# Products with v in four runs of two sets of heads a batch instead of eight runs of one

## The chip, the cores and the metric

The kernel runs on one core of one Trainium2 chip. The metric is device time of one execution in microseconds (us). The engines of the core are named as in the profile: PE is TensorE (PEld its loading of weights), DVE is VectorE, ACT is ScalarE, POOL is GpSimd, SP is the engine that issues the DMAs.

## The reference

Sixteen independent graphs ("batches") of 512 nodes with 128 features go through two layers, all in float32:

```python
h = relu(layernorm(x))                                 # per node
q, k, v = split(h @ W_qkv + b_qkv)                     # 8 heads of 16
scores = where(adj, q @ k.T / 4, -inf)                 # 512 x 512 a head
x = x + (softmax(scores) @ v) @ W_out + b_out          # layer 0
h = relu(layernorm(x))
z_l, z_g, v = h @ Wl, h @ Wg, h @ Wv
A_l = relu(cosine(z_l)); A_g = exp(-|z_g - z_g'|^2/2)  # zero diagonal
K = 0.9 * rownorm(A_l * adj) + 0.1 * rownorm(A_g * adj)
out = x + (K @ v) @ Wo                                 # layer 1
```

The change concerns `softmax(scores) @ v` of layer 0.

## The kernel before

**One time axis of slots.** The program of every engine is written out by one loop `for s in slots`. A batch takes 32 slots for its attention tiles (8 heads times 4 blocks of 128 nodes), and the other stages stand in a table `AT` by name, as slot numbers counted from the batch's own slot 0; batch b's are 32 b later. The table runs from slot -37 to slot 100, so in the steady state three or four batches are in work at a time. This text counts slots modulo 32, "slot 0" to "slot 31", and calls 32 slots a round. Within a slot the order of the stages on an engine is that of the code. Each engine is a queue in program order; the semaphores (`reached(...)`) say what it waits for. [...]

**A tile of attention.** In each slot PE makes one tile of scores (L725, read by DVE at L1021 for the maxima of the rows) and one tile of the same scores turned, 128 keys by 512 queries, of 21 slots ago (L733; in every slot divisible by 4 the mask is first put into that bank by L721). ACT takes the exponential of the turned tile into `probs_t` (L1186), and POOL multiplies three of four such tiles by the mask (L587). There are two banks for the scores and two for the turned tiles, so both matmuls of a slot wait until DVE and ACT have read those of two slots before.

**Sets and products with v.** Four turned tiles, of the four heads of a group and one block of keys, make a set. There are eight sets a batch: four blocks of keys for each of the two groups of heads. `attend` multiplies a set by v: four matmuls, one for each head, which write 32 of the 128 partitions each of the bank `pv_bank` and add up over the four sets of a group. In float32 each is two matmul instructions in the trace, so a set is 8 rows of L747. `probs_t` keeps six sets (`KEPT`). After the fourth set of a group ACT copies the bank (`pv_copy`, L1229). In the table, "pv" stands at eight slots of a batch, four apart: modulo 32 these are slots 28, 0, 4, 8 for the first group and 12, 16, 20, 24 for the second.

**Other work in these slots on PE.** Slot 28: `mix_cos` of the second layer (L761) and `yT` (L779), which turns the scaled y after DVE's `y_scale` (L1118). Slot 30: `mix_rbf` (L761), after DVE's `adj_rbf` (L1053), and `attn` (L895). Slot 0: `max_turn` (L854). Slot 4: nothing else. Slots 5, 6, 8, 10: `z` (L756), whose banks are those that DVE's `out` (L1062 to L1076) reads. Slots 8 and 10: q and k (L756), which ACT and DVE split into two parts (L1248, L1095). Slot 12: `zgT` (L779). Slot 13: nothing else. Slots 14 to 17: `col`, `zlT`, `rbf`, `cos`, from where DVE's masks of layer 1 start (`cos_read`, L1039). Slot 20: nothing else. Slot 27: `y` (L779), after DVE's first `y_scale`.

**The last batch** has its own slots for the second layer (`AT_LAST`); "pv" is not among them.

Of the kernel before, what the change touches and what calls it, by code (L numbers as in the profile page):

```python
# [53 lines left out]
AT = {  # L54

    "hT": (-26,), "q": (-24,), "k": (-22,), "v": (-13,), "max_turn": (17, 32),
    "pv": (28, 32, 36, 40, 44, 48, 52, 56), "y": (54, 59), "yT": (60,), "attn": (62,), "h2T": (66,),
    "z": (69, 70, 72, 74), "zgT": (76,), "col": (78,), "zlT": (79,), "rbf": (79, 83, 85, 87),
    "cos": (81, 83, 86, 90), "mix_cos": (92, 95, 97, 98), "mix_rbf": (94, 95, 97, 98),

# [37 lines left out]
def reached(engine, signal, batch, nth=None):  # L98
    count = (batch * signal.per + (signal.per if nth is None else nth)) * signal.step
    if count > 0:  # L100
        engine.wait_ge(signal.sem, count)


def graph_blocks(nc, x, adj, w_qkv, b_qkv, w_out, b_out, w_l, w_g, w_v, w_o, out):
# [3 lines left out]
    T = N // P  # L108
    GROUPS = 2
    HG = H // GROUPS  # L110
# [38 lines left out]
    def kept(batch, k):  # L149

        return (SETS * batch + k) % KEPT
# [8 lines left out]
    with ExitStack() as ctx:  # L160
        def sb(name, shape, dt=F32):
            return ctx.enter_context(nc.sbuf_tensor(name, shape, dt))

        def bank(name):
            return ctx.enter_context(nc.psum_tensor(name, [P, 512], F32))

        def signal(name, per=1, step=1):
            return Signal(ctx.enter_context(nc.semaphore(name)), per, step)
# [52 lines left out]
        v_cols = sb("v_cols", [P, 3, T, H, 32])  # L221
# [4 lines left out]
        probs_t = sb("probs_t", [P, KEPT, HG, N])  # L226
# [3 lines left out]
        yT = sb("yT", [P, N])  # L230
# [40 lines left out]
        pv_bank = bank("pv")  # L271
# [71 lines left out]
        pv_filled = signal("pv_filled", SETS)  # L343
# [322 lines left out]
        def _(pe):  # L666
# [67 lines left out]
                              qk_rows[row:row + ROWS + 2, b % 2, 0, h // 2, :], start=w not in by_pe, stop=True,  # L734
                              tile_position=(row, 0)).then_inc(turned_filled.sem, 1)

            def attend(b, k):
                g, j = divmod(k, T)
                ends = (k + 1) * HG
                reached(pe, probs_masked, b, sum(w < ends for w in by_pool))  # L740
                if by_pe:
                    reached(pe, probs_ready, b, 1 + max(w for w in by_pe if w < ends))
                if j == 0:
                    reached(pe, v_ready, b)
                    reached(pe, pv_copied, b, g)
                for hl in range(HG):
                    last = pe.matmul(pv_bank[32 * hl:32 * (hl + 1), :], v_cols[:, b % 3, j, g * HG + hl, :],  # L747
                                     probs_t[:, kept(b, k), hl, :], start=(j == 0), stop=(j == T - 1),
                                     tile_position=(0, 32 * hl))
                last.then_inc(pv_filled.sem, 1)  # L750

            def split_product(dst, left, right, before_rest=None):
                for part, (a, c) in enumerate(((0, 0), (0, 1), (1, 0))):
# [5 lines left out]
            def mix(bank_, adjacency, n, right, rows):  # L759
                for m in rows:  # L760
                    last = pe.matmul(bank_, adjacency[:, m, n * P:(n + 1) * P], right(m), start=(m == 0),  # L761
                                     stop=(m == T - 1))
                return last
# [10 lines left out]
            def rbf_half(batch, n):  # L774
                return mix_bank(batch, n)[:, 256:256 + D + 1]
# [6 lines left out]
            for s in slots:  # L782
# [11 lines left out]
                if hit := due(s, "pv"):  # L794
                    attend(*hit)

                if hit := due(s, "cos"):
                    b, m = hit
# [8 lines left out]
                if hit := due(s, "rbf"):  # L807
                    b, m = hit
# [10 lines left out]
                if hit := due(s, "mix_cos"):  # L819
                    b, n = hit  # L820
# [13 lines left out]
                if hit := due(s, "mix_rbf"):  # L834
                    b, n = hit
# [4 lines left out]
                    else:  # L840
                        m = n
                        reached(pe, rbf_ready, b, m + 1)
                        for n in range(T):
                            last = mix(rbf_half(b, n), adj_rbf, n, v_of_rbf, [m])
# [3 lines left out]
                if hit := due(s, "max_turn"):  # L848
                    b, g = hit
# [7 lines left out]
                if hit := due(s, "hT"):  # L857
                    b, _ = hit
# [3 lines left out]
                for which, name in enumerate(("q", "k")):  # L862
                    if hit := due(s, name):
                        b, _ = hit
# [7 lines left out]
                if hit := due(s, "v"):  # L872
                    b, _ = hit
                    reached(pe, hT_ready, b)
                    bank_free(pe, work_turns, b, "v")
                    for t in range(T):
                        last = pe.matmul(work_bank[:, t * P:(t + 1) * P], hT[:, t * P:(t + 1) * P],
                                         wqkv_sb[:, 2 * D:3 * D], start=True, stop=True)
                    last.then_inc(v_filled.sem, 1)
                if hit := due(s, "y"):  # L880
                    b, g = hit
# [3 lines left out]
                if hit := due(s, "yT"):  # L885
                    b, _ = hit
# [3 lines left out]
                if hit := due(s, "attn"):  # L890
                    b, _ = hit
                    reached(pe, yT_ready, b)
                    bank_free(pe, work_turns, b, "attn")
                    for t in range(T):
                        last = pe.matmul(work_bank[:, t * P:(t + 1) * P], yT[:, t * P:(t + 1) * P],  # L895
                                         wout_sb[:, :], start=True, stop=True)
                    last.then_inc(attn_filled.sem, 1)
                if hit := due(s, "h2T"):
                    b, _ = hit
# [3 lines left out]
                if hit := due(s, "z"):  # L903
                    b, t = hit
# [13 lines left out]
                if hit := due(s, "zgT"):  # L918
                    b, _ = hit
# [3 lines left out]
                if hit := due(s, "col"):  # L923
                    b, _ = hit
# [3 lines left out]
                if hit := due(s, "zlT"):  # L928
                    b, _ = hit
# [377 lines left out]
```

## Time and profile before

| | |
|---|---|
| three runs | 848.60, 844.22, 848.76 us (median 848.6) |
| profiled execution | 850.23 us, its span 848.5 us, 1.7 us around it |
| busy share of the span | PE 91%, DVE 79%, POOL 74%, ACT 69% |
| mean granted clock of TensorE | 0.971 of full speed |

All engines work side by side, and none is busy all the time. A busy PE in the profile counts matmuls whose ends are modelled, so the share alone does not tell what ends the time; the chain of waits does, and it goes through several engines in turn. The rounds of the steady state are alike: from about 140 us on, a round takes 48.25 us (from the matmul L725 of slot 28 at 385.28 us to that at 433.52 us), and the same waits come back in each.

### The profile page before, as it was taken

How to read it: one execution, taken by the hardware profiler on the slowest of the kernel's cores; microseconds unless marked ns; L12 is line 12 of the kernel's file. 1: busy time of each engine (PE TensorE's matmuls, PEld its weight loads, DVE VectorE, ACT ScalarE, POOL GpSimd, SP SyncE). 2: the span in 40 equal slices, each digit the busy share in tenths (PEclk: the TensorE clock that was granted, in tenths of full speed). 3: DMA queues.
4: the chain of work that ended last, by engine and by line, in shares of the span. 5: the costliest groups of instructions: out<-in, count | busy, mean ns of one | idle time of the engine just before them, and what ended most of it. 6: DMA issues, size and time to landing. Idle time of an engine off the chain costs nothing.

```text
span 848.5 us, 15592 instructions
## 1 busy us (share of the span) xinstructions
PE 774.0 (91%) x4736; PEld 410.8 (48%) x4736; DVE 672.5 (79%) x1957; ACT 589.5 (69%) x1230; POOL 624.4 (74%) x707
## 2 busy tenths in 40 slices
PE   4888799999999999999999999999999999989886
PEld 3322235546454554646454554645455454536366
DVE  6677659788887979788797979888796978877266
ACT  4337676876868686776868687776868677575832
POOL 3249786887869697886969788786969788685911
PEclk9859889999999999999999999999999999999999
DMA  2211111120201121020112112020112111100000
GB/s 87 69 56 58 33 57 33 32 70 20 82 16 55 33 65 38 29 73 20 53 30 69 33 37 65 20 82 20 51 32 70 32 34 57 32 2 2 13 1 26
DMA packets 43059, 35.76 MB, mean 42 GB/s; under 512 B 6625, under 2 KB 36834, under 8 KB 42978
## 3 DMA queue, kind: packets, MB, share of 16 engines
q1 hardware_dynamic: 42978, 34.76, 13.5%
q8 instruction: 41, 0.67, 0.3%
q14 instruction: 40, 0.33, 0.1%
HBM read 17.70 MB, written 16.78 MB: 41 GB/s over the span
## 4 chain that ended last, share of the span: by engine, by line
PE 59%; DVE 19%; ACT 12%; issue 7%; POOL 1%; DVEq 0%; POOLq 0%; ACTq 0%
PE adj L761 14%; PE score L725 11%; PE pv L747 10%; PE adj L756 7%; DVE scrap L1021 7%; PE work L779 6%; ACT probs_t L1186 4%; DVE adj_cos L1039 3%; PE turned L721 3%; DVE rbf_arg L1048 3%; DVE adj_rbf L1053 2%; PE work L756 2%; ACT zl_square L1264 2%; PE work L895 2%; ACT z L1257 2%
## 5 line engine op out<-in xcount | busy, mean ns | idle before, releaser
L587 POOL TENSOR_TENSOR probs_t<-probs_t,keep_t 128x512 int32<-128x512 int32 x384 | 488.7, 1300 | 70.8 <-ACT probs_t L1186 70.6
L1186 ACT ACTIVATE probs_t<-turned,exp_scale 128x512 f32<-128x512 f32 x512 | 345.1, 695 | 94.0 <-PE turned L733 91.2
L1021 DVE CUSTOM_DVE_ANT_0 scrap<-score,mask_add 128x512 f32<-128x512 f32 x512 | 340.3, 682 | 56.9 <-PE score L725 56.6
L725 PE MATMUL score<-qk_rows 48*128 48x512 f16 x512 | 193.4, 395 | 26.9 <-ACT probs_t L1186 20.3
L733 PE MATMUL turned<-qk_rows 50*128 50x512 f16 x512 | 192.6, 395 | 1.1 <-ACT probs_t L1186 1.1
L747 PE MATMUL pv<-probs_t,v_cols 128*32 128x512 f32 x1024 | 140.3, 621 | 1.3 <-POOL probs_t L587 1.3
L725 PEld LDWEIGHTS score<-qk_rows 48*128 48x128 f16 x512 | 44.1, 93 | 184.0 <-issue 114.9
L761 PE MATMUL adj<-v_cos,adj_cos 128*128 128x129 f32 x480 | 69.3, 286 | 0.4 <-DVE out_sb L1076 0.4
L761 PEld LDWEIGHTS adj<-v_cos,adj_cos 128*128 128x128 f32 x480 | 58.1, 190 | 21.9 <-issue 21.2
L761 PE MATMUL adj<-z,adj_rbf 128*128 128x129 f32 x480 | 64.7, 278 | 0.0
L1053 DVE SCALAR_TENSOR_TENSOR adj_rbf<-rbf_exp,mask_t 128x512 f32<-128x512 f32 x64 | 62.7, 982 | 1.0 <-ACT rbf_exp L1220 1.0
L756 PE MATMUL adj<-zgT_parts 128*128 128x512 f32 x186 | 59.2, 427 | 2.8 <-DVE zgT_parts L1139 1.0
L756 PE MATMUL adj<-zlT_parts 128*128 128x512 f32 x186 | 60.0, 431 | 1.7 <-DVE adj_cos L1039 0.6
L761 PEld LDWEIGHTS adj<-z,adj_rbf 128*128 128x128 f32 x480 | 58.1, 191 | 6.0 <-issue 6.0
L1220 ACT ACTIVATE rbf_exp<-rbf_arg,rbf_bias 128x512 f32<-128x512 f32 x64 | 45.9, 718 | 18.8 <-DVE rbf_arg L1048 16.9
L1048 DVE TENSOR_TENSOR rbf_arg<-adj,col_term 128x512 f32<-128x512 f32 x62 | 42.5, 685 | 18.2 <-PE adj L756 17.7
L721 PE MATMUL turned<-bar_t,ident_b 128*128 128x512 bf16 x128 | 50.7, 396 | 2.3 <-ACT probs_t L1186 1.4
L598 POOL TENSOR_SCALAR var_eps<-moments 128x4 f32<-128x4 f32 x16 | 3.6, 228 | 60.7 <-DVE moments L996 60.7
L733 PEld LDWEIGHTS turned<-qk_rows 50*128 50x128 f16 x512 | 43.7, 93 | 7.2 <-ACT probs_t L1186 3.6
L1039 DVE SCALAR_TENSOR_TENSOR adj_cos<-adj,mask_t 128x512 f32<-128x512 f32 x62 | 42.5, 686 | 4.5 <-PE adj L756 3.7
L756 PE MATMUL adj<-wz_parts,h2T_parts 128*128 128x384 f32 x180 | 44.6, 356 | 0.1
L1195 ACT ACTIVATE x_norm<-x_sb,ln_shift,rstd 128x128 f32<-128x128 f32 x64 | 26.4, 483 | 23.7 <-issue 18.6
(170 smaller groups left out, 1123.0 us busy)
## 6 DMA issues: line engine op xcount, KB each, us to landing
q_dram<-split SPq DMA_DIRECT2D x48, 128.0 KB, 2.1
k_dram<-split SPq DMA_DIRECT2D x48, 128.0 KB, 2.2
qk_rows<-q_dram SPq DMA_DIRECT2D x64, 96.0 KB, 2.7
qk_rows<-k_dram SPq DMA_DIRECT2D x64, 96.0 KB, 2.7
x_sb<-in_x_dram SPq DMA_DIRECT2D x16, 256.0 KB, 3.1
out_dram<-out_sb SPq DMA_DIRECT2D x15, 256.0 KB, 2.5
qk_rows<-max_rows SPq DMA_DIRECT2D x128, 2.0 KB
adj_sb<-in_adj_dram SPq DMA_DIRECT2D x1, 256.0 KB, 3.0
```

What stands on the lines that cost most here:

```text
L587: pool.tensor_tensor(tile, tile, keep_t[:, w // HG % T, :], ALU.mult).then_inc(probs_masked.sem, 1)
L721: pe.matmul(turned_bank[w % 2][:, :], ident_b[:, :], bar_t[:, w // HG % T, :], start=True, stop=False)
L725: pe.matmul(score_bank[u % 2][:, :], qk_rows[row:row + ROWS, b % 2, 0, h // 2, t * P:(t + 1) * P], qk_rows[row:row + ROWS, b % 2, 1, h // ...
L733: pe.matmul(turned_bank[w % 2][:, :], qk_rows[row:row + ROWS + 2, b % 2, 1, h // 2, j * P:(j + 1) * P], qk_rows[row:row + ROWS + 2, b % 2, ...
L747: last = pe.matmul(pv_bank[32 * hl:32 * (hl + 1), :], v_cols[:, b % 3, j, g * HG + hl, :], probs_t[:, kept(b, k), hl, :], start=(j == 0), ...
L756: last = pe.matmul(dst, left(a), right(c), start=(part == 0), stop=(part == 2))
L761: last = pe.matmul(bank_, adjacency[:, m, n * P:(n + 1) * P], right(m), start=(m == 0), stop=(m == T - 1))
L1021: dve.tensor_tensor_reduce(scrap[:, u % 2, :], score_bank[u % 2][:, :], mask_add[:, t, :], -1.0 / MAX_UNIT, 3.0e38, ALU.add, ALU.min, neg_ ...
L1039: dve.scalar_tensor_tensor(adj_cos[:, m, :], cos_bank(b, m)[:, :], 0.0, mask_t[:, m, :], ALU.max, ALU.mult).then_inc(cos_ready.sem, 1)
L1048: dve.tensor_tensor(rbf_arg[:, m % 2, :], rbf_bank(b, m)[:, :], col_term[:, :], ALU.add).then_inc(rbf_arg_ready.sem, 1)
L1053: dve.scalar_tensor_tensor(adj_rbf[:, m, :], rbf_exp[:, m % 2, :], 1.0, mask_t[:, m, :], ALU.min, ALU.mult).then_inc(rbf_ready.sem, 1)
L1186: act.activation(probs_t[:, kept(b, k), w % HG, :], turned_bank[w % 2][:, :], ACT.Exp, scale=exp_scale[:, 0:1]).then_inc(probs_ready.sem, 1)
```

## The change

"pv" stands at four slots of a batch instead of eight, and each call of `attend` multiplies two sets. The slots that stay are those of the second set of each pair, 0, 8, 16 and 24 modulo 32; slots 28, 4, 12 and 20 lose their set. The waits are those of the second set, and are made ahead of the first. The signal `pv_filled` still goes up once a set. Lines of the changed kernel below this place stand three lines further down (L747 becomes L750).

```diff
-    "pv": (28, 32, 36, 40, 44, 48, 52, 56), "y": (54, 59), "yT": (60,), ...
+    "pv": (32, 40, 48, 56), "y": (54, 59), "yT": (60,), ...
...
-            def attend(b, k):
-                g, j = divmod(k, T)
-                ends = (k + 1) * HG
+            def attend(b, pair):
+                g = 2 * pair // T
+                ends = 2 * (pair + 1) * HG
                 reached(pe, probs_masked, b, sum(w < ends for w in by_pool))
                 if by_pe:
                     reached(pe, probs_ready, b, 1 + max(w for w in by_pe if w < ends))
-                if j == 0:
+                if 2 * pair % T == 0:
                     reached(pe, v_ready, b)
                     reached(pe, pv_copied, b, g)
-                for hl in range(HG):
-                    last = pe.matmul(pv_bank[32 * hl:32 * (hl + 1), :], v_cols[:, b % 3, j, g * HG + hl, :],
-                                     probs_t[:, kept(b, k), hl, :], start=(j == 0), stop=(j == T - 1),
-                                     tile_position=(0, 32 * hl))
-                last.then_inc(pv_filled.sem, 1)
+                for k in (2 * pair, 2 * pair + 1):
+                    j = k % T
+                    for hl in range(HG):
+                        last = pe.matmul(pv_bank[32 * hl:32 * (hl + 1), :], v_cols[:, b % 3, j, g * HG + hl, :],
+                                         probs_t[:, kept(b, k), hl, :], start=(j == 0), stop=(j == T - 1),
+                                         tile_position=(0, 32 * hl))
+                    last.then_inc(pv_filled.sem, 1)
```

PE before, slots 4 to 8 of a round: `score` and `turned` are the two tiles of a slot, `turned<-bar_t` opens slots 4 and 8, `wz_parts` is `z`, `x_norm` is `hT`, and `wqk_parts` in slot 8 is q.

```order
L721 MATMUL turned<-bar_t,ident_b 128x512
L725 MATMUL score<-qk_rows 128x512
L733 MATMUL turned<-qk_rows 128x512
L747 MATMUL pv<-probs_t,v_cols 32x512 x4
L725 MATMUL score<-qk_rows 128x512
L733 MATMUL turned<-qk_rows 128x512
L756 MATMUL adj<-wz_parts,h2T_parts 128x384 x3
```

PE now at the same place, from slot 4 to the start of `z` in slot 5:

```order
L721 MATMUL turned<-bar_t,ident_b 128x512
L725 MATMUL score<-qk_rows 128x512
L733 MATMUL turned<-qk_rows 128x512
L725 MATMUL score<-qk_rows 128x512
L733 MATMUL turned<-qk_rows 128x512
L759 MATMUL adj<-wz_parts,h2T_parts 128x384 x3
```

The tiles of slots 4 and 5 now follow each other with nothing between them; the set that stood there is in slot 8, ahead of q.

PE now in slot 8 and after it: the run of two sets, q, `z`, and the tiles of slot 9.

```order
L721 MATMUL turned<-bar_t,ident_b 128x512
L725 MATMUL score<-qk_rows 128x512
L733 MATMUL turned<-qk_rows 128x512
L750 MATMUL pv<-probs_t,v_cols 32x512 x8
L759 MATMUL work<-hT_parts,wqk_parts 128x512 x3
L759 MATMUL adj<-wz_parts,h2T_parts 128x384 x3
```

Where `x8` stands there was `x4`; all else in the slot has kept its order, and stands behind four matmuls more.

PE before, slots 12 to 14: `work<-ident,z` is `zgT`, `work<-ident,rbf_bias` is `col` of slot 14.

```order
L733 MATMUL turned<-qk_rows 128x512
L747 MATMUL pv<-probs_t,v_cols 32x512 x4
L779 MATMUL work<-ident,z 128x128 x4
L725 MATMUL score<-qk_rows 128x512
L733 MATMUL turned<-qk_rows 128x512
L725 MATMUL score<-qk_rows 128x512
L733 MATMUL turned<-qk_rows 128x512
L779 MATMUL work<-ident,rbf_bias 128x128 x4
```

PE now at the same place:

```order
L733 MATMUL turned<-qk_rows 128x512
L782 MATMUL work<-ident,z 128x128 x4
L725 MATMUL score<-qk_rows 128x512
L733 MATMUL turned<-qk_rows 128x512
L725 MATMUL score<-qk_rows 128x512
L733 MATMUL turned<-qk_rows 128x512
L782 MATMUL work<-ident,rbf_bias 128x128 x4
```

Four matmuls are gone from slot 12; they are in slot 16, behind that slot's tiles and ahead of the `cos` of slot 17.

## Rows read from the trace of the kernel before

**Rows 1.** The page, parts 4 and 5: the chain by line; L747's group.

```profile
PE adj L761 14%; PE score L725 11%; PE pv L747 10%; PE adj L756 7%; DVE scrap L1021 7%; PE work L779 6%; ACT probs_t L1186 4%; DVE adj_cos L1039 3%; PE turned L721 3%; DVE rbf_arg L1048 3%; DVE adj_rbf L1053 2%; PE work L756 2%; ACT zl_square L1264 2%; PE work L895 2%; ACT z L1257 2%
...
L747 PE MATMUL pv<-probs_t,v_cols 128*32 128x512 f32 x1024 | 140.3, 621 | 1.3 <-POOL probs_t L587 1.3
```

**Rows 2.** Chain of waits, 384 to 436 us: start, length (us), what.

```profile
384.30 0.14 issue
...
385.67 0.99 PE pv L747 x8
...
393.55 1.00 PE pv L747 x8
...
400.60 0.99 PE pv L747 x8
...
405.04 0.99 PE pv L747 x8
...
406.96 0.03 ACT split L1248
...
417.32 0.99 PE pv L747 x8
...
419.57 0.69 DVE adj_cos L1039
...
432.11 0.44 DVE y_sb L1118
```

**Rows 3.** PE in order of time: start, length (us), what, [idle before <-releaser].

```profile
387.59 0.60 PE L779 MATMUL work<-ident,y_sb 128*128 128x128 f32 x4
...
388.66 1.16 PE L761 MATMUL adj<-z,adj_rbf 128*128 128x129 f32 x8
...
393.48 1.07 PE L747 MATMUL pv<-probs_t,v_cols 128*32 128x512 f32 x8
394.36 0.22 PE L854 MATMUL work<-ident_h,max_parts 128*32 128x128 f16 x1
...
403.30 0.77 PE L756 MATMUL adj<-wz_parts,h2T_parts 128*128 128x384 f32 x3
...
405.96 0.96 PE L756 MATMUL work<-hT_parts,wqk_parts 128*128 128x512 f32 x3
...
414.16 0.37 PE L725 MATMUL score<-qk_rows 48*128 48x512 f16 x1 [1.24 <-ACT probs_t L1186]
...
418.25 0.39 PE L725 MATMUL score<-qk_rows 48*128 48x512 f16 x1
...
430.17 0.39 PE L725 MATMUL score<-qk_rows 48*128 48x512 f16 x1
```

**Rows 4.** DVE in order of time, the same round.

```profile
386.31 0.42 DVE L1118 TENSOR_TENSOR y_sb<-work,inv_den 128x256 f32<-128x256 f32 x1
...
387.26 0.68 DVE L1053 SCALAR_TENSOR_TENSOR adj_rbf<-rbf_exp,mask_t 128x512 f32<-128x512 f32 x1
...
402.59 0.35 DVE L1076 SCALAR_TENSOR_TENSOR out_sb<-adj,inv_degree,half_sum 128x128 f32<-128x128 f32 x1
...
431.22 0.68 DVE L1021 CUSTOM_DVE_ANT_0 scrap<-score,mask_add 128x512 f32<-128x512 f32 x1
```

**Rows 5.** POOL in order of time, the same round.

```profile
391.05 1.28 POOL L587 TENSOR_TENSOR probs_t<-probs_t,keep_t 128x512 int32<-128x512 int32 x1
```

**Rows 6.** Windows of the round before: length, busy time (count) by engine, PEclk, DMA.

```profile
363.40:366.60 3.20, 1.96 (x12) 1.02 (x12) 1.91 (x5) 2.63 (x8) 2.96 (x5) 0.99 0.63 205
366.60:370.00 3.40, 3.40 (x14) 1.50 (x16) 2.29 (x5) 2.31 (x4) 3.23 (x7) 0.50 0.00 0
```

**Rows 7.** PE in order of time, the same stretch of that round.

```profile
364.94 0.37 PE L725 MATMUL score<-qk_rows 48*128 48x512 f16 x1 [1.24 <-ACT probs_t L1186]
...
370.58 0.39 PE L725 MATMUL score<-qk_rows 48*128 48x512 f16 x1
```

More of the change, by code:

```diff
@@ L56 @@
     "hT": (-26,), "q": (-24,), "k": (-22,), "v": (-13,), "max_turn": (17, 32),
-    "pv": (28, 32, 36, 40, 44, 48, 52, 56), "y": (54, 59), "yT": (60,), "attn": (62,), "h2T": (66,),
+    "pv": (32, 40, 48, 56), "y": (54, 59), "yT": (60,), "attn": (62,), "h2T": (66,),
     "z": (69, 70, 72, 74), "zgT": (76,), "col": (78,), "zlT": (79,), "rbf": (79, 83, 85, 87),
```

## The prediction

> **What bounds the kernel now.** I read the chain of waits first, then each engine in order of time over one round (slot 28 at 385.28 us to the next slot 28 at 433.52 us, 48.25 us), then the windows.
>
> The chain by line gives the products with v 10% of the span, 85 us [rows 1]. A set stands on the chain with 0.99 us [rows 2], and there are 1024 / 8 = 128 sets [rows 1], so 127 us if all stood there. About 86 of 128 do, some five in eight, and the chain of the round shows which: those at 385.67, 393.55, 400.60, 405.04 and 417.32 us, that is of slots 28, 0, 4, 8 and 16 [rows 2]. The sets of slots 12, 20 and 24 stand beside the chain. What takes their place is to be seen in the same view: from 406.96 us the chain is ACT (the split of q, then z, exponentials and squares one after the other) until PE's tile of slot 14 at 414.16 us, for which PE had stood idle 1.24 us [rows 2, 3]; from 419.57 us it is DVE, from the first `cos_read` to `y_scale` at 432.11 us [rows 2]; then PE again, from slot 27 to q of slot 8. So the round is a relay: PE in slots 27 to 8, ACT in 8 to 13, PE in 14 to 17, DVE in 17 to 27.
>
> **The change part by part.** I follow one round and keep an account of how much later (+) or earlier (-) the chain is than before.
>
> *A run of two sets.* No run of two is in the trace. A set that is followed by a matmul of its own tile shape (`max_turn`, 128*32) gives way after 394.36 - 393.48 = 0.88 us; the other sets, followed by another shape, after 0.99 us [rows 2, 3]. The second set could cost nothing if it lay wholly beside the first, and 0.99 us if it gained nothing; I take 0.88, the nearest row. A doubled slot is then 0.88 us longer, and a slot that loses its set 0.99 us shorter, if PE has something to do.
>
> *Pair of slots 28 and 0.* Without its set, PE reaches `yT` 0.99 us earlier, at 386.60. But y comes from DVE, at 386.31 + 0.42 = 386.73 [rows 4], and from an engine's end to PE's start the chain has 0.14 us [rows 2]: 386.87 instead of 387.59, -0.72. `mix_rbf` of slot 30 would then start at 387.94, but `adj_rbf` ends at 387.26 + 0.68 = 387.94 and lets it go at 388.08 instead of 388.66 [rows 3, 4]: -0.58. DVE runs on from slot 25 without a gap there, so it does not come earlier. In slot 0 POOL's last mask ends at 391.05 + 1.28 = 392.33 [rows 5]; PE is there at 393.48 - 0.58 = 392.90, no wait. Then the second set: -0.58 + 0.88 = **+0.30**.
>
> *Pair of slots 4 and 8.* Slot 4 is left with its tiles. PE would now reach the second `z` (slot 6) 0.7 us earlier, but its bank is read by `out`, which ends at 402.59 + 0.35 = 402.94 [rows 4] and is itself 0.30 later, since DVE had waited for the score of slot 3. `z` starts at 402.94 + 0.30 + 0.14 = 403.38 instead of 403.30 [rows 3]: +0.08. Of 0.99 us taken away, PE gets 0.22. In slot 8 q then starts at +0.08 + 0.88 = **+0.96**, 406.92 instead of 405.96 [rows 3]. The split of q on ACT and all that follows it in ACT's queue, up to the exponential that frees the tile of slot 14, comes 0.96 later.
>
> *Pair of slots 12 and 16.* The set of slot 12 lay in time in which PE then waits for ACT anyway. Taking it out makes the wait of 1.24 us [rows 3] about 2.2 us, and the tile of slot 14 comes no earlier. The second set in slot 16 stands ahead of `cos`, on the chain: +0.88, together **+1.84**.
>
> *Pair of slots 20 and 24.* From `cos_read` to `y_scale` DVE is the chain, so taking the set of slot 20 out gives nothing. The second set in slot 24 lets the score of slot 25 start at 430.17 + 0.88 = 431.05 [rows 3] instead; it takes 0.39, so DVE can't start on it before 431.44, where it started at 431.22 [rows 4]: +0.22, and `y_scale`, behind it in DVE's queue, as much. Together **+2.06 us a round**. ACT's copy of the bank comes 0.88 later and pushes the exponentials of slots 25 and 26; that falls behind the wait for `y_scale` in slot 28, where PE waits anyway.
>
> *Waits that the change adds or moves.* The wait for masks is that of the second set, which was met at the same slot before; sets waited 1.3 us for POOL in all [rows 1]. The first set's tiles are held four slots longer, and ACT wants their place of six back thirteen slots or more after the new run: no wait. No DMA is moved; those of the maxima follow `max_turn`, later by as much as the chain.
>
> Fifteen rounds at 2.06 us are 30.9 us. The sixteenth is split between start and end, where fewer batches overlap; its four pairs lie between -0.11 and +0.88 each, -0.4 to +3.5 us, and I count nothing.
>
> *The clock.* In the round before, PE stood idle 1.24 us ahead of slot 14 [rows 7], was busy 1.96 of 3.20 us around it, and the granted clock then was 0.50, 1.2 instead of 2.4 GHz, for the next 3.40 us [rows 6]. From the tile of slot 14 to that of slot 17 that round took 370.58 - 364.94 = 5.64 us, the round at full clock 418.25 - 414.16 = 4.09 [rows 3, 7]: a fall costs 1.55 us, and this stretch is PE's part of the chain. The round of rows 3 had the same idle time and no fall, so before it stands at the edge. With about 2.2 us of idle time at this place I expect it in most rounds, and count ten more: 15.5 us (none to fifteen more: 0 to 23 us). The Trainium skill ("TensorE: Matmul & The Clock Gate", Part 1) says that the clock is granted by how busy PE has lately been, and these rows agree; by that rule the idle time that a longer wait adds is paid twice.
>
> Sum: 850.2 us of the profiled execution (848.5 of span and 1.7 around it) + 30.9 + 15.5 = 896.6. That execution lies 1.6 us above the median of the runs, so in their terms 848.6 + 46.4 = **895 us**.
>
> **The rivals.**
>
> *Only the waits, no more falls of the clock:* 848.6 + 30.9 = 880. For it: in the round of the other rows the same wait of 1.24 us passed at full clock [rows 3]. Against: the wait grows by three quarters.
>
> *The waits are smaller than I think:* sets taken from slots 28 and 4, which are on the chain, pay in full (0.99 against 0.88, -0.11 each), and only the sets that move from beside the chain onto it cost: 0.88 + 0.22 - 0.22 = 0.88 a round, 13 us, 862. For it: a DVE that is not held up may run ahead. Against: `y_scale` and `out` end when they end, in queues without gaps.
>
> *Every moved set costs its full price:* 4 x 0.88 x 15 = 53, with 23 of clock 925. For it: each doubled slot is followed by work that others wait for. Against: the slack computed in slots 28, 4 and 25.
>
> *Faster:* one place and price, the exit from a run of sets into another shape of tile. Four exits fewer a batch, 64 in all, at 0.99 - 0.88 = 0.11 us [rows 2, 3] are 7 us: 842. It decides if PE has its next operands ready wherever a set is taken away, so in slots 28, 4, 12 and 20 alike. The Trainium skill ("TensorEngine Tiling (Array Packing)", Key Properties) says that a change of tiling mode drains the engine; the 0.11 us agrees, and by this rule alone the time would be 842. Against it: three of eight sets, with two of those taken away, lie where PE waits for ACT or DVE, and a drain saved there is waited away.
>
> **How the numbers follow.** Forecast 0.55 (895, own range 884 to 912), waits alone 0.20 (880, 872 to 888), smaller waits 0.10 (862), full price 0.07 (925), faster 0.05 (842), about no change 0.03. A measurement of this kernel tells half a per cent, 4 us, from no change. The range 863 to 914 leaves out the two ends, half of the smaller waits and the edges: under 0.2. Faster 0.05, within half a per cent 0.02, slower 0.93.
>
> **What would show it.** In the profile of the changed kernel: a set's rows in pairs, some 1.87 us from a run's start to the next shape; PE's idle time ahead of the tile of slot 14 near 2.2 us and again due to ACT's exponential; a wait for `y_sb` at `yT` and for `out_sb` ahead of the second `z`; the chain still through DVE from `cos_read` to `y_scale`; a round of about 50.3 us, 51.9 with a fall of the clock, and a mean clock near 0.94. It would be wrong if the round came out under 49 us, if the sets of slots 0 or 8 came off the chain, or if PE's idle time in slot 13 stayed at 1.2 us.

## The result, and the profile after

The changed kernel takes 896.0 us (median of four runs, 893.98 to 897.98) where the kernel before, run beside it, takes 847.7 (844.22 to 848.76): a ratio of 1.060, 95% interval 1.056 to 1.063, 48.3 us slower. Forecast were 895 us. The sum was near, in part by luck: the waits of a round were taken 0.6 us too high, and the start and end of the execution, which hold more waits than were counted for them, made it good, as the traces and runs below show. The profiled execution took 894.96 us, its span 893.2, 44.7 us more than that of before, at a mean clock of 0.951 (0.971 before).

First the page of the changed kernel: the clock in 40 slices, the chain by engine and by line, and the group of the products with v.

```profile
PEclk9968999999999999999999999999999999989899
...
PE 72%; ACT 12%; issue 6%; DVE 5%; POOL 1%; SPq 0%; DMA 0%; DVEq 0%; POOLq 0%; ACTq 0%
...
L750 PE MATMUL pv<-probs_t,v_cols 128*32 128x512 f32 x1024 | 127.1, 616 | 2.1 <-POOL probs_t L587 2.1
```

The same two lines of the page of the kernel before, which do not stand above:

```profile
PEclk9859889999999999999999999999999999999999
...
PE 59%; DVE 19%; ACT 12%; issue 7%; POOL 1%; DVEq 0%; POOLq 0%; ACTq 0%
```

DVE has left the chain (19% to 5%), and PE has taken its place. The products with v hardly wait for POOL (2.1 us in all, 1.3 in [rows 1]). The slices of the clock hide what the windows below show: most read 9, though the clock falls in every steady round.

The chain of waits of the changed kernel, one round: start, length (us), what.

```profile
410.04 1.85 PE pv L750 x16
...
422.28 1.85 PE pv L750 x16
...
425.06 0.03 ACT split L1251
...
436.95 1.85 PE pv L750 x16
...
440.05 0.70 DVE adj_cos L1042
...
449.10 1.85 PE pv L750 x16
```

All four runs of two sets stand on the chain whole, 7.4 us a round, where five sets with 0.99 us stood there before [rows 2]. The `adj_cos` at 440.05 is the only work of DVE left on the chain of the round; before, DVE was the chain from there to `y_scale`. ACT's stretch from the split of q to the tile of slot 14 is still there.

PE of the changed kernel in order of time, from one slot 28 to the next: start, length (us), what, [idle before <-releaser].

```profile
402.64 0.39 PE L725 MATMUL score<-qk_rows 48*128 48x512 f16 x1 [0.42 <-ACT probs_t L1189]
...
402.96 1.16 PE L764 MATMUL adj<-v_cos,adj_cos 128*128 128x129 f32 x8
404.03 0.63 PE L782 MATMUL work<-ident,y_sb 128*128 128x128 f32 x4
...
409.97 1.92 PE L750 MATMUL pv<-probs_t,v_cols 128*32 128x512 f32 x16
411.71 0.22 PE L857 MATMUL work<-ident_h,max_parts 128*32 128x128 f16 x1
...
418.33 0.37 PE L725 MATMUL score<-qk_rows 48*128 48x512 f16 x1 [0.39 <-ACT probs_t L1189]
...
420.44 0.77 PE L759 MATMUL adj<-wz_parts,h2T_parts 128*128 128x384 f32 x3
...
422.21 1.92 PE L750 MATMUL pv<-probs_t,v_cols 128*32 128x512 f32 x16
424.06 0.96 PE L759 MATMUL work<-hT_parts,wqk_parts 128*128 128x512 f32 x3
...
430.00 0.63 PE L782 MATMUL work<-ident,z 128*128 128x128 f32 x4 [0.90 <-DVE split L1098]
...
432.25 0.37 PE L725 MATMUL score<-qk_rows 48*128 48x512 f16 x1 [1.25 <-ACT probs_t L1189]
...
438.74 0.39 PE L725 MATMUL score<-qk_rows 48*128 48x512 f16 x1
...
453.84 0.39 PE L725 MATMUL score<-qk_rows 48*128 48x512 f16 x1 [0.42 <-ACT probs_t L1189]
```

The round is 453.84 - 402.64 = 51.20 us, 2.95 more than the 48.25 before. Twelve rounds of the trace are alike in this; together they take 614.4 us, the same twelve of the kernel before 579.7. That is 34.7 of the 44.7 us by which the span grew; the other 10.0 lie in the start and the end. A run of two is left after 424.06 - 422.21 = 1.85 us, and after 1.74 when `max_turn` follows: the second set costs 0.86. Idle time that was not there before stands ahead of the tile of slot 5 (0.39, at 418.33), which waits for an exponential of ACT, and ahead of `zgT` in slot 12 (0.90), which waits until DVE's split of k has read the bank that `zgT` writes. The 1.25 ahead of slot 14 are what they were [rows 3].

The 0.42 ahead of the tile of slot 28 are for the most part no wait. The mask matmul L721 of that slot stands in them; its own row is missing, as are 74 of 128 in this trace, while its weight load is there:

```profile
L721 PEld LDWEIGHTS turned<-bar_t,ident_b x128: 95/96/151, 51.9 to 850.7; 128*128 128x128 bf16 x128
L721 PE MATMUL turned<-bar_t,ident_b x54: 376/390/634, 52.0 to 850.7; 128*128 128x512 bf16 x54
...
402.30 0.10 PEld L721 LDWEIGHTS turned<-bar_t,ident_b 128*128 128x128 bf16 x1 [0.33 <-DVE neg_max L1024]
```

The work before it ends at 402.22, so what PE waits there is about 0.1 us.

From the tile of slot 14 to that of slot 17 it is 438.74 - 432.25 = 6.49 us against 4.09 [rows 3], and the windows of the changed kernel tell why: length, busy time (count) of PE, PEld, DVE, ACT, POOL, then the clock, DMA share and GB/s.

```profile
429.00:433.20 4.20, 2.05 (x16) 1.13 (x14) 3.11 (x9) 3.68 (x13) 3.00 (x5) 1.00 0.50 164
433.20:436.60 3.40, 3.40 (x13) 1.96 (x12) 1.50 (x5) 2.15 (x4) 2.90 (x5) 0.50 0.12 33
436.60:440.00 3.40, 3.40 (x24) 1.08 (x24) 2.05 (x7) 1.57 (x3) 2.94 (x5) 1.00 0.01 2
```

PE is busy 2.05 of 4.20 us, and then has half its clock for 3.40 us, in the stretch in which it is the chain. This comes in each of the twelve rounds, 51.2 us apart; in the profile of the kernel before it comes in one of the twelve. Of the 2.40 us, 0.88 are the added set and 1.52 the clock.

By slot, a round of the changed kernel against one before, median of the steady rounds (us; a slot's time runs from its turned tile on PE to that of the next slot, and slots that are not named differ by less than 0.05): 28: -0.89, 0: +0.86; 4: -0.54, 6: +0.32, 7: +0.11, 8: +0.85; 12 to 14: 0; 15: +1.51, 16: +0.89; 20: -0.41, 23: -0.21, 24: +0.86, 25: -0.34, 27: -0.06. These numbers are called the account below.

### The profile page after: what moved, and what is told of

It is laid out like the page before. It is cut to its first block, busy times and chain, and to the rows that moved or that the text cites. A ratio compares the mean times of both kernels' runs of the same rounds, so it can differ in the third digit from the quotient of the medians.

```text
span 893.2 us, 15452 instructions
## 1 busy us (share of the span) xinstructions
PE 772.3 (86%) x4660; PEld 428.9 (48%) x4736; DVE 664.5 (74%) x1957; ACT 591.2 (66%) x1230; POOL 618.4 (69%) x707
## 4 chain that ended last, share of the span: by engine, by line
PE 72%; ACT 12%; issue 6%; DVE 5%; POOL 1%; SPq 0%; DMA 0%; DVEq 0%; POOLq 0%; ACTq 0%
PE adj L759 15%; PE pv L750 14%; PE adj L764 13%; PE score L725 12%; PE work L782 7%; ACT probs_t L1189 4%; PE work L759 2%; PE turned L721 2%; DVE scrap L1024 2%; PE work L898 2%; ACT zl_square L1267 2%; ACT z L1260 1%; PE work L880 1%; PE turned L733 1%; DVE adj_cos L1042 1%
## 5 line engine op out<-in xcount | busy, mean ns | idle before, releaser
L587 POOL TENSOR_TENSOR probs_t<-probs_t,keep_t 128x512 int32<-128x512 int32 x384 | 481.9, 1278 | 125.1 <-ACT probs_t L1189 123.5
L750 PE MATMUL pv<-probs_t,v_cols 128*32 128x512 f32 x1024 | 127.1, 616 | 2.1 <-POOL probs_t L587 2.1
L759 PE MATMUL adj<-zgT_parts 128*128 128x512 f32 x186 | 68.2, 481 | 1.3 <-DVE zgT_parts L1142 1.0
L750 PEld LDWEIGHTS pv<-probs_t,v_cols 128*32 128x32 f32 x1024 | 27.4, 112 | 59.4 <-issue 55.4
L1056 DVE SCALAR_TENSOR_TENSOR adj_rbf<-rbf_exp,mask_t 128x512 f32<-128x512 f32 x64 | 53.1, 832 | 1.0 <-ACT rbf_exp L1223 1.0
L759 PEld LDWEIGHTS adj<-zgT_parts 128*128 128x128 f32 x186 | 36.5, 219 | 19.7 <-issue 9.7
```

What stands on the lines that cost most here:

```text
L587: pool.tensor_tensor(tile, tile, keep_t[:, w // HG % T, :], ALU.mult).then_inc(probs_masked.sem, 1)
L759: last = pe.matmul(dst, left(a), right(c), start=(part == 0), stop=(part == 2))
L1056: dve.scalar_tensor_tensor(adj_rbf[:, m, :], rbf_exp[:, m % 2, :], 1.0, mask_t[:, m, :], ALU.min, ALU.mult).then_inc(rbf_ready.sem, 1)
```

## The experiments

All experiments have a table `PV_RUNS`, which says what sets each call of `attend` multiplies, and `attend` loops over that run as the changed kernel loops over its pair. Ratios are against the kernel before on the same chip, which took 845.7 to 846.3 us there.

### The four pairs, each alone

```diff
-    "pv": (28, 32, 36, 40, 44, 48, 52, 56),
...
+    "pv": (32, 36, 40, 44, 48, 52, 56),    # p1_pair_28_0:   runs (0, 1) (2,) (3,) (4,) (5,) (6,) (7,)
+    "pv": (28, 32, 40, 44, 48, 52, 56),    # p2_pair_4_8:    runs (0,) (1,) (2, 3) (4,) (5,) (6,) (7,)
+    "pv": (28, 32, 36, 40, 48, 52, 56),    # p3_pair_12_16:  runs (0,) (1,) (2,) (3,) (4, 5) (6,) (7,)
+    "pv": (28, 32, 36, 40, 44, 48, 56),    # p4_pair_20_24:  runs (0,) (1,) (2,) (3,) (4,) (5,) (6, 7)
```

Slots 28 and 0:

> Only the sets of slots 28 and 0 become one run in slot 0; the other six sets stay single. By the account of the prediction (y_scale and adj_rbf hold PE in slots 28 and 30) the round grows by 0.30 us, 15 rounds, so 852 us against 847.7. By the round measured with all four pairs (slots 28 to 1 took 9.23 us before and after) it costs nothing: 848. If the four pairs share the loss of 48 us evenly: 860. The clock should fall no more often than before.

848.56 us, ratio 1.002 (0.9999 to 1.005); the round 48.42, that is +0.20: slot 28 -0.68, slot 0 +0.86. The added set costs its 0.86, the one taken away pays 0.68.

Slots 4 and 8:

> Only the sets of slots 4 and 8 become one run in slot 8. By the account of the prediction +0.66 us a round: 858 us. By the round measured with all four pairs (slot 1 to q of slot 8 took 0.74 us longer) 859. If the loss is shared evenly: 860. If the drain saved is what counts: 846. PE's idle time ahead of slot 14 stays 1.24 us, so the clock falls in few rounds.

861.5 us, ratio 1.017 (1.012 to 1.021); the round 48.97, +0.75: slot 4 -0.54, 6 +0.31, 7 +0.11, 8 +0.85. Of the set taken away 0.12 us is left by slot 8. The account of the changed kernel has the same four numbers.

Slots 12 and 16:

> Only the sets of slots 12 and 16 become one run in slot 16. The set of slot 12 lies where PE waits for ACT. By the account of the prediction +0.88 us a round, and PE's idle time ahead of slot 14 grows to some 2.2 us, so the clock falls in nearly every round at 1.5 us each: 847.7 + 13 + 22 = 883 us. Without falls of the clock 861. If the loss is shared evenly: 860.

883.34 us, ratio 1.043 (1.037 to 1.049); the round 51.22, +3.0. It alone makes the clock fall in eleven of the twelve rounds, and longer than in the changed kernel. Windows of this experiment, the same columns:

```profile
423.20:426.60 3.40, 1.72 (x11) 0.74 (x9) 2.20 (x6) 3.40 (x13) 2.36 (x3) 0.97 0.32 111
426.60:430.00 3.40, 2.93 (x10) 1.66 (x11) 1.77 (x5) 2.14 (x5) 3.07 (x8) 0.50 0.42 125
430.00:433.40 3.40, 3.40 (x17) 1.51 (x20) 2.35 (x5) 1.78 (x3) 2.19 (x4) 0.53 0.00 0
```

By slot: 14 +0.68, 15 +1.53, 16 +1.32, 23 -0.21, 25 -0.34. Take away the set (0.88), and 2.65 us of clock are left, one time and three quarters the 1.52 of the changed kernel. That the time is the 883 of the expectation is luck: the clock costs more than the 1.5 us that it had, and slots 23 and 25 give 0.55 back, which it had not. The first two `adj_rbf` after `cos_read` take 1.31 and 0.68 us here; why that matters is shown below.

Slots 20 and 24:

> Only the sets of slots 20 and 24 become one run in slot 24. By the account of the prediction (DVE is the chain there, the score of slot 25 comes too late for it) +0.22 us a round: 851 us. By the round measured with all four pairs (slots 17 to 28 took 0.17 us less) 845. If the loss is shared evenly: 860. The clock should fall no more often than before.

855.7 us, ratio 1.010 (1.006 to 1.014); the round 48.71, +0.49: 20 -0.40, 22 +0.38, 24 +0.86, 25 -0.34, 27 -0.06. No account had this: that of the prediction had too little, and 860 was too much. In the changed kernel the same slots make -0.17. The set taken out of slot 20 gives nothing here, as the prediction had it, for nearly all of its 0.40 goes into slot 22 again; the second set in slot 24 costs 0.46 where 0.22 were foreseen. PE and DVE of this experiment show a wait for DVE in slot 22:

```profile
425.20 0.63 PE L783 MATMUL work<-ident,pv_sb 128*128 128x128 f32 x4 [0.19 <-DVE v_cols L1109]
```

```profile
421.20 1.56 DVE L1057 SCALAR_TENSOR_TENSOR adj_rbf<-rbf_exp,mask_t 128x512 f32<-128x512 f32 x1
...
423.29 1.16 DVE L1057 SCALAR_TENSOR_TENSOR adj_rbf<-rbf_exp,mask_t 128x512 f32<-128x512 f32 x1
```

The four alone add up to 4.44 us a round, together they cost 2.95. Two causes for the difference stood to be tried, the clock and these long `adj_rbf`.

### The clock held up

Five matmuls on constants fill PE's idle time ahead of the tile of slot 14, once in the changed kernel, once in the kernel before. They write a bank that is free there, and nothing reads what they write.

```diff
+    "warm": (77,),
...
+                if (hit := due(s, "warm")) and hit[0] < B - 1:
+                    for _ in range(5):
+                        pe.matmul(adj_bank[0][:, :], ident_b[:, :], mask_add[:, 0, :], start=True, stop=True)
```

> The changed kernel with five extra matmuls a batch in slot 13, of constants into a bank that nobody reads before it is written anew; they lie in PE's wait for ACT ahead of the tile of slot 14 (about 1.1 of 1.25 us) and change no result. If the falls of the clock cost 1.5 us in each round, as the stretch from slot 14 to 17 has it, the clock stays up, the round takes 49.7 us instead of 51.2 and the kernel about 896 - 22 = 874 us. If the falls only fill time in which PE would wait anyway, 896.

874.23 us, ratio 1.034 (1.031 to 1.037). The page's clock, and PE at the place:

```profile
PEclk9968999999999999999999999999999999999999
```

```profile
420.89 0.63 PE L783 MATMUL work<-ident,z 128*128 128x128 f32 x4 [0.90 <-DVE split L1102]
421.50 0.37 PE L726 MATMUL score<-qk_rows 48*128 48x512 f16 x1
421.51 0.39 PE L734 MATMUL turned<-qk_rows 50*128 50x512 f16 x1
421.83 1.25 PE L803 MATMUL adj<-mask_add,ident_b 128*128 128x512 bf16 x5
423.14 0.37 PE L726 MATMUL score<-qk_rows 48*128 48x512 f16 x1
```

With the 1.25 us filled, and the 0.90 still there, the clock falls in no steady round, and the round is 49.67 us; the rest of the account is unchanged. The falls of the changed kernel so cost 896.0 - 874.2 = 21.8 us.

> The kernel before with the same five matmuls in slot 13. Its clock falls there in one or two rounds of an execution, at 1.5 us each: 1 to 3 us less than before, 843 to 845 against 845.9, which may be no difference that can be measured. If the extra matmuls delay the tile of slot 14, slower by up to 15 x 0.5 us.

842.64 us, ratio 0.996 (0.994 to 0.998), 3.7 us less: the falls of the kernel before were worth so little, since few of its rounds had one.

The four times together part the loss. With the clock held in both kernels the change costs 874.2 - 842.6 = 31.6 us, which are waits; the falls that it adds cost 21.8 - 3.7 = 18.1 us. By the spans of the four profiled executions (893.2, 869.3, 848.5, 841.4) it is 27.9 and 16.8; the runs of the changed kernel with the clock held spread from 871.0 to 877.7 us, and its profile is of the shortest. Of the 27.9 us of waits the twelve alike rounds hold 17.2 (596.1 against 578.9 us, 1.44 a round). The other 10.7 lie in the start and the end; what makes them was not taken apart, and as the two kernels differ there by 6.7 us at half clock, a part of them can be clock.

### Who makes DVE late

Taking two of POOL's multiplications by the mask out, those beside the first two `adj_rbf` after `cos_read`, from the kernel before, and from that with the pair 20 and 24 alone (these two kernels leave out a part of the computation):

```diff
-    by_pool = [w for w in range(SLOTS) if w % HG not in MASK_BY_PE]
+    by_pool = [w for w in range(SLOTS) if w % HG not in MASK_BY_PE and w not in (29, 30)]
```

DVE and POOL of the kernel before, the stretch that the experiment is about:

```profile
422.62 1.56 DVE L1053 SCALAR_TENSOR_TENSOR adj_rbf<-rbf_exp,mask_t 128x512 f32<-128x512 f32 x1
...
424.71 1.15 DVE L1053 SCALAR_TENSOR_TENSOR adj_rbf<-rbf_exp,mask_t 128x512 f32<-128x512 f32 x1
```

```profile
422.34 1.29 POOL L587 TENSOR_TENSOR probs_t<-probs_t,keep_t 128x512 int32<-128x512 int32 x1
423.57 1.74 POOL L587 TENSOR_TENSOR probs_t<-probs_t,keep_t 128x512 int32<-128x512 int32 x1
425.55 1.46 POOL L587 TENSOR_TENSOR probs_t<-probs_t,keep_t 128x512 int32<-128x512 int32 x1 [0.24 <-ACT probs_t L1186]
```

> The kernel before, with two of POOL's multiplications by the mask left out in each batch (the tiles of slots 18 and 19, so one block of keys of two heads stays unmasked): those that run beside DVE's first two adj_rbf, which take 1.56 and 1.15 us there instead of 0.69. If POOL's work stretches them, they fall to 0.7 us; DVE's stretch is 1.3 us shorter, and PE, whose own waits in slots 22 to 27 come to some 0.6 us, gains about 0.6 us a round: 837 us. If DVE's stretch doesn't bound the round: 846, with the short adj_rbf.

837.45 us, ratio 0.991 (0.988 to 0.994); the round 47.66: slot 23 -0.21, slot 25 -0.34. DVE of this experiment:

```profile
413.60 0.68 DVE L1057 SCALAR_TENSOR_TENSOR adj_rbf<-rbf_exp,mask_t 128x512 f32<-128x512 f32 x1
...
415.03 0.69 DVE L1057 SCALAR_TENSOR_TENSOR adj_rbf<-rbf_exp,mask_t 128x512 f32<-128x512 f32 x1
```

> The run of two in slot 24 alone (855.7 us), with the same two multiplications left out. In the kernel with all four pairs this pair cost nothing, alone it costs 0.49 us a round, by a wait of 0.38 us in slot 22. If the difference is the stretched adj_rbf, this wait goes and slot 23 gets shorter too: some 0.6 us a round less, 846 us. If not, 856.

847.65 us, ratio 1.003 (0.9997 to 1.005); the round 48.08. The +0.38 of slot 22 is gone and the -0.21 of slot 23 is there, as in the changed kernel. There DVE reads:

```profile
443.10 1.30 DVE L1056 SCALAR_TENSOR_TENSOR adj_rbf<-rbf_exp,mask_t 128x512 f32<-128x512 f32 x1
...
444.94 0.68 DVE L1056 SCALAR_TENSOR_TENSOR adj_rbf<-rbf_exp,mask_t 128x512 f32<-128x512 f32 x1
```

The rounds of the kernel before, of p4, x1 and x2 are 48.23, 48.72, 47.67 and 48.08 us. So the two masks cost 0.56 us a round without the pair and 0.64 with it, and the pair 20 and 24 costs 0.49 with the masks and 0.41 without them: it has a price of its own, which the masks do not explain. What the changed kernel has beside it is the gain of x1: its slots 23 and 25 read -0.21 and -0.34 as there, and its `adj_rbf` take 1.30 and 0.68 us. The pair 12 and 16, which alone has the same two steps and 1.31 and 0.68, brings that gain. With the two steps counted there, the pair 20 and 24 costs -0.41 + 0.86 - 0.06 = +0.39 in the changed kernel, as it does in x2.

A fall of the clock brings the same gain to the kernel before. In its one steady round with a fall [rows 6, 7] slots 15 and 16 take 1.55 us longer, slots 23 and 25 take 0.54 less, and `adj_rbf` 1.32 and 0.68 us. The tile of slot 28 ahead of that round stands here:

```profile
336.06 0.39 PE L725 MATMUL score<-qk_rows 48*128 48x512 f16 x1
```

The round is 385.28 - 336.06 = 49.22 us, 0.99 more than those beside it and not 1.55. In x1, where there is nothing left to give back, the one steady round with a fall takes 49.20 instead of 47.67 us, 1.53 more.

### Is there a better place for a set?

If sets only have to stand where PE waits anyway, moving one from the chain into such a place should pay. Set 3 from slot 8 to slot 9, where PE waits for ACT's split; set 5 from slot 16 to slot 20, where DVE seemed to be the chain:

```diff
-    "pv": (28, 32, 36, 40, 44, 48, 52, 56),
...
+    "pv": (28, 32, 36, 41, 44, 48, 52, 56),    # f1_set3_slot9
+    "pv": (28, 32, 36, 40, 44, 52, 56),        # f2_set5_slot20: runs (0,) (1,) (2,) (3,) (4,) (5, 6) (7,)
```

> The kernel before with the set of slot 8 one slot later, in slot 9, so behind q instead of ahead of it; all runs single. If ACT's stretch from q to the tile of slot 14 is the chain, as read from the chain of waits, it starts 0.99 us earlier, PE has room for the set ahead of k, and the round shrinks by up to 0.99 us: 833 us. If PE's own work is what bounds the round, moving a set by one slot changes nothing: 846.

841.49 us, ratio 0.995 (0.992 to 0.997); the round 47.97, 0.26 less, a quarter of the full gain. By slot: 8 -0.35, 9 +1.10, 10 -0.63, 13 -0.21, 23 -0.18. The chain of this experiment names what is late next:

```profile
403.75 0.49 ACT hT L1240
...
404.33 0.70 DVE hT_parts L1092
405.04 0.14 issue
405.17 0.94 PE work L760 x3
```

q now waits for its own operand. The set of slot 8 had covered that.

> The kernel before with the set of slot 16 moved to slot 20, where it makes a run of two with the set that stands there. So a run of two sets in a slot beside the chain, and a set less on PE's stretch ahead of the cos of slot 17, from where DVE is the chain. If that reading holds, up to 0.9 us a round less: 833 us. If runs of two cost by themselves, or DVE's stretch isn't the chain: 846 or more.

846.1 us, ratio 1.001 (0.999 to 1.004); the round 48.37, +0.14. The gain did not come: slot 16 -0.51, 17 +0.28, 19 +0.08, 20 +0.86, 23 -0.21, 25 -0.34. PE of this experiment at slot 17:

```profile
414.58 0.39 PE L726 MATMUL score<-qk_rows 48*128 48x512 f16 x1 [0.42 <-DVE neg_max L1025]
...
415.17 0.96 PE L760 MATMUL adj<-zlT_parts 128*128 128x512 f32 x3 [0.21 <-DVE zlT_parts L1148]
```

PE got half of the set back in slot 16, having to wait for DVE, and lost more of it in slot 17. In slot 20, where I had taken it to be free, the set cost 0.86, of which slots 23 and 25 gave 0.55 back: PE, being later, waited less for DVE there.

Last, two changes on top of set 3 in slot 9: three constant matmuls in slot 13, and with them one of the masks beside `adj_rbf` given from POOL to PE.

```diff
-    by_pe = [w for w in range(SLOTS) if w % HG in MASK_BY_PE]
-    by_pool = [w for w in range(SLOTS) if w % HG not in MASK_BY_PE]
+    by_pe = [w for w in range(SLOTS) if w % HG in MASK_BY_PE or w in (30,)]
+    by_pool = [w for w in range(SLOTS) if w not in by_pe]
```

> The set of slot 8 in slot 9 and three extra matmuls in slot 13, masks as before: what the candidate has without the mask by PE. The round of the set alone was 47.97 us against 48.22, without a fall of the clock in the steady part; so 841, or 0.5 us a round more if the extra matmuls delay the tile of slot 14: 848.

841.19 us, ratio 0.994 (0.992 to 0.997): the filler alone adds nothing measurable to f1.

> Candidate for a faster kernel: the set of slot 8 in slot 9, three extra matmuls in slot 13 to hold the clock, and the mask of the tile of slot 19 put in by PE (0.32 us more there) instead of POOL, so that POOL is done 1.3 us earlier beside adj_rbf. The set alone gave 841.5. DVE's stretch gets about 0.5 us shorter, PE's work 0.3 us longer: 838 us. If PE's work is what counts there: 845.

838.76 us, ratio 0.990 (0.988 to 0.994): 1% faster than the kernel before, and the fastest of those that leave nothing of the computation out. Against the kernel without the mask by PE, that mask costs 0.42 us in slot 18 and gives 0.15 and 0.34 back in slots 19 and 25; the round is 47.87 instead of 47.97 us.

## Why the prediction came out, step by step

The prediction had four pairs and a clock. A round (us), after less before; the steps of slots 23 and 25 have a row of their own:

| | predicted | alone | in the changed kernel |
|---|---|---|---|
| 28 and 0 | +0.30 | +0.20 | -0.03 |
| 4 and 8 | +0.66 | +0.75 | +0.74 |
| 12 and 16, the second set | +0.88 | +0.88 (taken) | +0.89 |
| slots 23 and 25 | nothing | -0.55 (with 12 and 16) | -0.55 |
| 20 and 24 | +0.22 | +0.49 | +0.39 |
| sum of the waits | 2.06 | 1.77 | 1.44 |
| clock, of a round with a fall | 1.55 | 2.65 | 1.51 |

**Right: the cost of a second set.** 0.88 was taken, and 0.85 to 0.89 was measured in slots 0, 8, 16 and 24, alone and together.

**Right: slots 4 and 8.** DVE of the changed kernel has the `out` that the second `z` waits for:

```profile
419.94 0.35 DVE L1079 SCALAR_TENSOR_TENSOR out_sb<-adj,inv_degree,half_sum 128x128 f32<-128x128 f32 x1
```

It ends at 420.29, and `z` starts 0.15 us later, at 420.44, as foreseen; before, `z` started 0.36 us after it [rows 3, 4]. The wait of 0.39 for ACT's exponential in slot 5 stands ahead of it and was not foreseen. Of 0.99 us PE kept 0.12 instead of 0.22.

**Right in the sum, wrong in the place: slots 12 and 16.** The prediction let the idle time ahead of slot 14 grow to 2.2 us, and named an idle time that stays at 1.2 as a sign of being wrong. It stayed at 1.25. What grew is the wait ahead of `zgT`, 0.90 us, in slot 12; the sum of the two, 2.15, is what was foreseen. The set of slot 12 had stood where DVE's split of k was awaited. Since ACT sets when slot 14 starts, the time is the same by both.

**Missing: DVE's `adj_rbf` beside POOL's masks.** The prediction took DVE's stretch from `cos_read` to `y_scale` to be as long as before, whatever PE does. It is not: two `adj_rbf` there took 1.56 and 1.15 us beside POOL's masks, and where the stretch starts at another time against the masks they take 1.30 and 0.68. This is worth 0.55 us a round, nearly all of the 0.62 by which the sum was too high. It is also a good part of why DVE left the chain, which the prediction had it keep: DVE has 19% of the chain before, 10% in x1 without the two masks, 13% in p4 with the pair 20 and 24, 5% in x2 with both, and 5% in the changed kernel.

**Wrong in size: slots 28 and 0.** "DVE runs on from slot 25 without a gap there, so it does not come earlier" holds for the pair alone, where +0.20 was measured, and fails in the changed kernel, where DVE comes 0.2 us earlier against PE for its shorter `adj_rbf`. The foreseen wait for `y_sb` at `yT` is there, but small: `yT` stands 1.07 us behind `mix_cos`, which took 1.00 before. ACT's copy of the bank pushes the exponential of slot 28, which costs about 0.1 us; the prediction laid that beside a larger wait for `y_scale`.

**Wrong in size: slots 20 and 24.** "From `cos_read` to `y_scale` DVE is the chain, so taking the set of slot 20 out gives nothing" holds for the pair alone. There the second set cost 0.46 instead of 0.22. With the shorter `adj_rbf` the first half fails too: taking the set out gives 0.41, and the second set costs its full 0.86. Why the 0.22 was too small by half when the pair stands alone was not taken apart.

**The clock: price right, count near.** A fall cost 1.52 us in the changed kernel where 1.55 was taken from one row [rows 3, 7]. That row's round lost 0.99 only, as the gain in `adj_rbf` came with the fall; in the changed kernel that gain is there with or without it, so the falls cost their full price. Ten more were counted. Between 120 us and the last 10 us of the execution the clock falls 15 times in the profile of the changed kernel and 3 times in that of before, 12 more. The runs have 18.1 us for it against 15.5.

**The whole sum.** The waits were put at 30.9 us, and the runs have 31.6 (27.9 by the spans). That they agree is luck: over the twelve alike rounds the prediction has 24.7 us and the traces 17.2. The start and the end, for which it has the other three rounds, 6.2 us, hold 10.7 by the spans. "I count nothing" for what lies outside fifteen rounds failed by 4 us by the spans and 8 by the medians; the rounds were overrated by 7.5.

Of the rivals, waits alone is what c1 brings about: 874, against 842.6 + 30.9 = 873.5 over a kernel before with its clock held too. Smaller waits (862) was right that DVE may run ahead, and wrong that slot 4 pays in full. Full price (925) fell, as only the pair 12 and 16 cost it in full. The faster one, four exits saved, fell: the exits are saved (1.85 us for two sets instead of 2 x 0.99), but slots 4, 12 and 20 pay back 0.12, nothing and 0.41 of the set that they lose.

## What to carry to other kernels

A short matmul group that depends on nothing recent can hide a wait where it stands. In this kernel, bunched sets cost their full time in the new place (0.85 to 0.89 us each time), and the place that they left paid back between nothing and 0.89, depending on what was late next. Before moving one, look in the order of time for that second wait, on each engine, and for the idle time that is left to PE: two waits of about one us a round were enough to pay for them again with half the clock. Where a sum comes near the result, check its terms by slot before trusting them; here the waits of the alike rounds were 7 us too high, and the start and the end made it good. And count how many rounds are alike before multiplying: there were twelve, not fifteen.

## What the runs showed of the hardware that was not expected

- DVE's `adj_rbf`, which reads two operands from SBUF, takes 0.68 to 0.69 us with no mask of POOL beside it [rows 4]; the first two after `cos_read` take 1.56 and 1.15 us in the kernel before and 0.68 and 0.69 in x1, without the masks. POOL waits too: the mask between those two takes 1.74 us and the one after it 1.46, where one alone takes 1.28 [rows 5]. In c1 the first `adj_rbf` takes 0.70 us, and the mask that runs on beside it 1.71. The Trainium skill ("SBUF — State Buffer", Who interferes with whom) says that a DVE instruction with two SBUF inputs and a GpSimd instruction that reads SBUF exclude each other. The rows of the kernel before agree: the mask that runs when the first `adj_rbf` starts at 422.62 has 1.01 us left, and with the 0.68 of `adj_rbf` itself a full wait would make 1.69, where 1.56 is measured.
- The longest idle time of PE does not tell by itself whether the clock falls here. 1.25 us with 0.90 just before it gave a fall in every steady round, 0.90 us alone (c1) in none, and 1.24 alone [rows 3, 6, 7] in one round and not in another. Why the pair 12 and 16 alone keeps the clock down for 6.8 us in most rounds, and the whole change for 3.4, was not tried and stays open.
